# Attention layers and experts on one core: new issue orders, and layer 1 chunk by chunk across tiles

## The reference

```python
# 4 graphs, 512 nodes, 8 heads of 64, 4 experts
def gat_layer(x, adj, W, a_self, a_neigh, b):
    feat = jnp.einsum('nf,hfo->hno', x, W)
    e = leaky_relu(attn_self[:, :, None] + attn_neigh[:, None, :], 0.2)
    e = e + MASK_VAL * (1.0 - adj)[None, :, :]          # MASK_VAL = -1e10
    alpha = jax.nn.softmax(e, axis=-1)
    out = jnp.einsum('hnm,hmo->hno', alpha, feat) + b[:, None, :]
    return elu(out transposed to [n, h*o])
x = x + vmap(gat_layer twice)(ctx_512, layernorm(x))    # adj is the layer norm of x, [4, 512, 512]
x4 = layernorm(x).reshape(B, G, E, H)                   # row n goes to expert n % 4
gate, up = split(einsum('bgeh,ehd->bged', x4, gate_up_proj))
x = x + einsum('bgei,eih->bgeh', silu(gate) * up, down_proj).reshape(B, N, H)
```

## Time and profile before

| what | us |
|---|---|
| three runs | 219.91, 219.63, 218.56 |
| median | 219.63 |
| profiled execution, first to last instruction | 217.7 |
| PE busy in it | 204.2 |
| mean granted PE clock in it | 0.983 |

### The profile page before, as it was taken

The page is one execution under the profiler, slowest core; times in us unless marked ns, Lnnn a source line. Parts: engine busy times, 40 slices in busy tenths (PEclk is TensorE's granted clock), DMA queues, the critical chain, the costliest instruction groups (busy, mean ns, idle before and its releaser), DMA issues.

```text
span 217.7 us, 2718 instructions
## 1 busy us (share of the span) xinstructions
PE 204.2 (94%) x890; PEld 160.1 (74%) x890; DVE 151.1 (69%) x298; ACT 103.3 (47%) x159; POOL 102.7 (47%) x82
## 2 busy tenths in 40 slices
PE   7897899959999999999999999999999999999990
PEld 2346677836788888888888888888888888888860
DVE  0769999738999853999967857999788651610140
ACT  3899999958967431132183044762353032112100
POOL 2000968398887768897079110786044502202200
PEclk9999999979999999999999999999999999999996
DMA  6999879444552859779996446734991200230024
GB/s 209 335 427 401 271 251 403 167 96 97 102 135 29 213 117 241 107 139 176 260 382 234 161 176 227 249 155 117 336 376 42 98 0 0 82 114 0 0 83 120
DMA packets 15203, 38.80 MB, mean 178 GB/s; under 512 B 2768, under 2 KB 2768, under 8 KB 14160
## 3 DMA queue, kind: packets, MB, share of 16 engines
q1 hardware_dynamic: 12080, 34.10, 43.6%
q0 software_dynamic: 2816, 4.20, 13.1%
q10 hardware_dynamic: 288, 0.26, 0.4%
HBM read 30.16 MB, written 8.40 MB: 177 GB/s over the span
## 4 chain that ended last, share of the span: by engine, by line
PE 78%; DVE 8%; ACT 7%; POOL 2%; issue 1%; DMA 1%; ACTq 0%; POOLq 0%
PE bank L1696 30%; PE bank L1710 15%; PE bank L1657 10%; PE bank L1632 10%; PE bank L1683 5%; PE bank L1646 3%; PE bank L1620 2%; ACT hexp L933 2%; DVE found L1256 2%; DVE hexp L1227 2%; DVE top L1252 2%; DVE val L1246 2%; PE bank L1740 2%; ACT hexp L939 1%; DMA y_table<-val 1%
## 5 line engine op out<-in xcount | busy, mean ns | idle before, releaser
L1696 PE MATMUL bank<-acts,ring 128*128 128x512 f32 x288 | 67.2, 390 | 0.0
L1696 PEld LDWEIGHTS bank<-acts,ring 128*128 128x128 f32 x288 | 53.9, 188 | 11.1
L1632 PE MATMUL bank<-wide,acts 128*128 128x512 f32 x192 | 49.1, 409 | 5.3 <-POOL acts L801 2.4
L1632 PEld LDWEIGHTS bank<-wide,acts 128*128 128x128 f32 x192 | 36.2, 191 | 17.6 <-issue 5.0
L795 POOL TENSOR_TENSOR ring<-ring_raw,ring 128x1024 fp32r<-128x1024 f32 x13 | 32.2, 2491 | 31.8 <-ACT ring L926 31.8
L1710 PE MATMUL bank<-ring,wide 128*128 128x512 f32 x144 | 34.7, 392 | 0.0
L926 ACT CAST ring<-ring_raw 128x1024 fp32r<-128x1024 f32 x24 | 24.7, 1056 | 17.0 <-DMA ring_raw<-in_down_t 10.9
L1710 PEld LDWEIGHTS bank<-ring,wide 128*128 128x128 f32 x144 | 26.8, 188 | 5.3
L820 POOL DMA_INDIRECT x_sb<-y_table,ff_row x16 | 25.1, 1569 | 4.5 <-issue 3.9
L1657 PE MATMUL bank<-ring,first_xnT 128*128 128x512 f32 x96 | 23.2, 394 | 0.0
L1307 DVE TENSOR_TENSOR hexp<-bank,hexp 128x512 f32<-128x512 f32 x12 | 8.2, 684 | 20.7 <-PE bank L1696 20.7
(11 more groups left out here) (86 smaller groups left out, 243.6 us busy)
## 6 DMA issues: line engine op xcount, KB each, us to landing
ring_raw<-in_gate_up_t SPq DMA_DIRECT2D x16, 512.0 KB, 5.8
x_sb<-in_x SPq DMA_DIRECT2D x4, 1024.0 KB, 10.0
ring_raw<-in_down_t SPq DMA_DIRECT2D x8, 512.0 KB, 5.5
y_table<-val SPq DMA_DIRECT2D x16, 256.0 KB, 3.4
out<-x_sb SPq DMA_DIRECT2D x16, 256.0 KB, 2.8
val<-in_x SPq DMA_DIRECT2D x4, 1024.0 KB
ctxT<-in_ctx_t SPq DMA_DIRECT2D x4, 256.0 KB, 5.2
wide_raw<-in_W_t SPq DMA_DIRECT2D x2, 512.0 KB, 7.0
```

The lines of the kernel that those rows point to most:

```text
L1632: last = nc.tensor.matmul(bank[Y_BANK[n]][:, :], hT[:, b % 2, c, w, t * P:(t + 1) * P], W1p[:, c, v, :], start=False, stop=(c == KC - 1 an ...
L1696: last = nc.tensor.matmul(bank[(UP_BANK if half else GATE_BANK)[KC * e + c]][:, :], ring[:, r % RING, w, col:col + P], xnT[:, (e - 1) % 2, ...
```

## The change

Nothing is added to or taken from the work: each engine has the same computing instructions and transfers as before, in a new order, with other waits and banks. (An unused helper, `keep_on`, goes.) What moves:

- SP loads `ctx` 1, both halves of W1 and b1 first, then x and the ring slots mixed, and all nine slots, all of x and all of `ctx` are issued before `store_y(0)`. The re-reads of the check are spread otherwise between the later ring loads.
- ACT runs `w_high(1)`, `seed(0)`, `w_high(2)` ahead of the first `h_exp_of`. DVE runs both `w_low` ahead of its first `h_below`.
- PE issues layer 1 by `layer1_part`, chunk by chunk with up to four tiles open at a time, and the waits on `w_lo` and `h_lo` move out of `layer1_part` to the list.
- The first expert's calls come in another order: `first_up` and `first_down` earlier, `turn_xn` singly between matmuls.
- All bank tables change, and the count of sure rows goes to `SURE_BANK` 5.

```diff
-        Z_BANK = (7, 1, 4, 3, 2, 1, 5, 3, 7, 1, 0, 2, 0, 4, 7, 5)
-        Y_BANK = (6, 4, 6, 5, 3, 4, 1, 5, 7, 6, 1, 2, 7, 2, 1, 2)
+        Z_BANK = (0, 2, 3, 4, 5, 6, 0, 2, 3, 4, 4, 1, 7, 4, 1, 2)
+        Y_BANK = (1, 7, 5, 6, 0, 1, 7, 2, 5, 6, 0, 3, 7, 4, 1, 2)
...
             load_ctx(0)
+            load_ctx(1)
             load_w(1)
-            load_ctx(1)
+            load_b1(0)
+            load_w(2)
+            load_x(2)
             load_ctx(2)
-            load_b1(0)
+            load_x(0)
+            load_r(1)
             load_x(1)
-            load_w(2)
-            load_x(0)
             load_r(0)
-            load_x(2)
+            load_x(3)
+            load_r(3)
+            load_r(5)
+            load_ctx(3)
+            load_r(2)
             load_r(8)
-            load_r(1)
-            load_r(2)
+            load_r(7)
+            load_r(4)
+            load_r(6)
             store_y(0)
-            load_r(7)
-            load_r(5)
-            load_r(6)
             store_y(1)
             store_f(0)
             store_y(2)
-            load_r(4)
             store_y(3)
-            load_r(3)
-            load_ctx(3)
-            load_x(3)
+            store_f(1)
...
             h_low(1, 3)
-            r_low(2)
-            h_low(2, 0)
             follow(0, 0)
             follow(0, 1)
+            follow(1, 0)
+            h_low(2, 0)
             follow(0, 2)
+            r_low(2)
             gather(0, 0)
+            r_low(4)
             h_low(2, 3)
             gather(0, 1)
-            r_low(4)
-            follow(1, 0)
+            h_low(3, 0)
+            gather(1, 0)
+            h_low(3, 1)
...
+            w_high(1)
+            seed(0)
+            w_high(2)
             h_exp_of(0, 0)
-            w_high(1)
             h_exp_of(0, 1)
...
+            w_low(1)
+            w_low(2)
             h_below(0, 0)
             h_value(0, 0)
-            w_low(1)
             h_below(0, 2)
...
                 if c == 0:
                     pe.wait_ge(y_seeded, n + 1)
-                if t == 0:
-                    wait_h_lo(pe, KC * b + c)
-                if n == 0 and c % 2 == 0:
-                    pe.wait_ge(w_lo, 1 + c // 2)
...
             layer0(1, 0)
-
+            layer0(1, 1)
+            pe.wait_ge(h_made, 1)
+            layer0(1, 2)
             pe.wait_ge(h_made, 2)
-            layer0(1, 1)
-            layer0(1, 2)
-
+            layer0(1, 3)
+            pe.wait_ge(h_made, 3)
+            layer0(2, 0)
+            pe.wait_ge(w_lo, 1)
+            wait_h_lo(pe, 0)
             layer1_part(0, 0)
+            layer1_part(1, 0)
+            wait_h_lo(pe, 1)
+            layer1_part(1, 1)
             pe.wait_ge(h_made, 4)
-            layer0(1, 3)
+            layer0(2, 1)
             layer1_part(0, 1)
...
```

More of the change, by code:

```diff
@@ L766, in _ @@
             load_r(22)
-            again_x(3)
             load_r(23)
@@ L1088, in _ @@
+            r_high(4)
+            y_exp_of(7)
+            h_exp_of(3, 0)
             h_high(2, 2)
[L1089 removed]
+            h_below(3, 0)
             h_high(2, 3)
[L1091 to L1103 removed]
```

770 lines of the change are left out of this document (417 added, 353 removed).

## The result

The changed kernel takes 235.03 us (median of 4 runs, 234.31 to 236.33) against 219.09 of the kernel before on the same chip: ratio 1.074, 95% interval 1.068 to 1.080. It is 16 us slower. The profiled execution is the slowest of the four, 236.33 us; its span is 234.5 us (before 217.7), its mean granted clock 0.95 (before 0.983).

The account below looks back on a forecast made before the run. PE was taken as the bound, with 10.1 us lost, nearly all before 50 us. Profiled span 217.7 minus 3.9 us of gain (clock falling at the start) gave 213.8; plus 1.9 us carried over, 215.7 us, range 212.8 to 220.8.

Parts of the forecast that it names:

- The change behind 68 us: Experts' stage after layer 1: work comes 4 us earlier, its feeders keep up with margins of 0 to 1 us.
- the sum of these: Net cost of the small margins in the experts' stage: zero, with up to 2 us in the range.
- 115.0 against 114.7 to 116: Experts' stage: r_low(9) behind x2_inverse(3, 2) comes at 115.0 us, PE reaches it at 114.7 to 116.
- rival (c): A late feeder of the experts, likeliest output(1, 0) before 148.9 us, gives the gain back: 217.5 to 219.6 us; chance 0.2.
- The front: Kernel start: PE stands 3.8 us, until 13.8, for h_value(0, 0) behind both W1 halves, whose second lands at 10.2.
- The fall of the clock: Behind the first PE gap: 3.1 to 3.3 us at half rate, of which 1.3 us are really lost.
- 14 to 49 us: Layer 1 chunk by chunk: small waits of 0.2 us to 38, 0 to 0.3 us for h_low(2, 0), old gap gone.
- rival (d): Early weight loads delay the f_row 1 store, PE stands 5 us and the clock falls: 222.5 us; chance 0.16.
- 49 to 68 us: Rest of layer 1: low halves come before PE needs them; it ends at 66.9, or 68.2 with the clock.
- 0.6 us on chunk (3, 3): Layer 1: DVE's h_low takes twice as long beside a POOL step, some 0.6 us, leaving 0.3 us of margin.
- 10.1 us is all that any order can give: Whole kernel: PE uses 206.9 us for 196.8 us of work, so reordering can win at most 10.1 us.
- rival (b): Start loads beat the walk, W1 landing at 9 instead of 10.2: 1.2 us more gain, 213 us; chance 0.08.

Follow-up runs that it names:

- experiment 7: Experiment 1 with x2_stats(2, 0) moved behind normalize(1, 2) on DVE: 224.96 us, ratio 1.026.
- experiment 6: Changed kernel with 44 small dummy matmuls on PE in the first gap to hold the clock up: 234.82 us, ratio 1.071.
- experiment 1: Changed kernel with only all_maxima moved back to its old place behind r_low(12) on POOL: 226.59 us, ratio 1.032.
- experiment 4: Changed kernel with r_low(4) behind h_low(2, 3) on POOL: uneven runs of 231.57, 231.92, 235.61 and 236.43 us.
- experiment 9: Experiments 1, 4 and 7 together, with r_low(9) and r_low(10) also ahead of x2_inverse(2, 2) again: 228.04 us, ratio 1.035.
- experiment 16: Kernel before the change with h_low(2, 3) ahead of follow(0, 2) and gather(0, 0) on POOL: 218.23 us, ratio 0.995.
- experiment 17: Experiment 16 plus x2_stats(0, 0) behind y_value(8) on DVE and both h_low(3, ...) ahead of gather(1, 1) on POOL: 219.03 us, ratio 1.000.
- experiment 5: Changed kernel with both W1 halves behind the first chunks again on ACT and DVE, loads as changed: 233.98 us, ratio 1.069.
- experiment 12: Experiment 11 with ACT's and DVE's first steps also put back as in experiment 5: 225.85 us, ratio 1.032.
- experiment 14: Experiment 12 with gather(0, 1) between h_low(2, 3) and r_low(4) on POOL: 224.15 us, ratio 1.022.
- experiment 11: Changed kernel with experiments 1, 4 and 7 together, r_low(9) left where the change put it: 221.94 us, ratio 1.011.

## Why the prediction was wrong

It said 215.7 us (212.8 to 220.8) and 0.67 for faster; it is 235.03 and slower. The failed step is "The change behind 68 us", and in it the sentence "I put the sum of these at zero and up to 2 us in the range": 14.9 us were lost there, 0.5 in the kernel before.

- **`all_maxima`** was never priced, though the move stands in the diff and the two holes in POOL's timeline of the kernel before (5.80 us "issue" in front, everything behind covered by a wait for ACT). Seen from PE it cost nothing there, and what covered it was not looked at. Undoing it alone gives 8.4 us, replacing the instruction 6.7.
- **`x2_stats(2, 0)`** ahead of `normalize(0, 3)` stands in front of a wait of 1.83 us; that it costs them is not shown, since moving it alone only moved the wait (experiment 7). **`r_low(9)`** behind `x2_inverse(3, 2)` cost 1.81 us once it was exposed. For `r_low(9)` the prediction had its margin as 115.0 against 114.7 to 116. Two waits of this size are rival (c)'s kind, but not at the place where it looked, and no row names `output(1, 0)`.
- **The clock behind the third gap:** 4.5 us at 0.50, in which PE loses 2.3 us, a wait of 0.43 among them. The prediction had no term for it there.
- **The front** had the right mechanism and a wrong size: gap until 13.8 predicted, 15.16 measured; 5.3 us lost predicted, 7.5 measured at 22 us. W1's second half landed at 11.65, not 10.2: bytes queued ahead of it were the only term, between two landings of the earlier trace rows. An earlier landing would not have helped either: `seed(0)` stands ahead of `w_high(2)` and needs b1, which landed at 10.3, and the bias row and the seed kept ACT busy until 11.64; the prediction had no term for these 1.3 us of work. The fall of the clock was right, its price nearer 2 us than 1.3 (experiment 6). Fronts with the same lists differ by up to 2 us between executions (lost at 22 us: 7.5, 7.8, 6.0, 6.2 and 7.9 in the changed kernel and experiments 1, 4, 7 and 9), so this term wanted a range of 2 us by itself.
- **14 to 49 us** went as walked: no wait for a `seed`, `w_lo` or `h_lo`, 7.5 to 7.6 us lost. The old wait at 44 us is gone, `h_low(2, 0)` behind `follow(1, 0)` costs nothing, and rival (d), loads ahead of `f_row`, did not happen.
- **49 to 68 us** failed at chunk (2, 2). The prediction had the mechanism, put it at 0.6 us on chunk (3, 3) and kept the sum. DVE's operation took 4.7 times its length (3.15 us), PE waited 2.34 us and then ran at the low clock. The prediction treated the overlap as a slow-down by two, when the operation can be held until two POOL instructions in a row are through.
- **The accounting**, "10.1 us is all that any order can give", nearly all of it lost before 50 us, was right as a bound and wrong as a forecast. In the kernel before, experiments 16 and 17 win 2.1 us by 46 us and 4.1 us by 61 us and keep 0.6 and 0.5. In the changed kernel the traces of experiments 4 and 5 keep what they won by the end of layer 1 (4.8 and 1.8 us), but other runs of the same lists are slower, and the medians are only 1.3 and 1.0 us lower. Undoing the front beside the other repairs even cost time (experiments 12 and 14 against 11), though 2.3 us less were lost at 22 us (6.4 and 4.1 in experiments 11 and 12): by the end of layer 1 experiments 11 and 14 both stand at 7.6.
- **The range.** Half-way from the forecast of 215.7 to rival (d)'s 222.5 is 219.1, not 220.8, and rival (b) gives 213.2, not 212.8. Neither changes the outcome.

What stays open: 2.5 us of the 16 (experiment 11 is still 1.1% slower), of which 1.8 are the wait for `r_low(9)`, behind the `x2_inverse` on POOL; the spread between runs of one list; and what makes the hole in front of a reduction 5.6 us long or 11.7. That `all_maxima` at the new place in the kernel before does the same was not tried: there `small_maxima` stands behind `normalize(2, 2)` on DVE, and the two would wait for each other.

## What to carry to other kernels

Before a step is moved, list on its engine what surrounds it in the trace, "issue" holes included, and ask what hides them at the old place and who waits right behind the new one; a call that cost PE nothing may have taken 14 us of a queue that nobody needed. Where several orders were moved together, undo them with their partners (a load, its cast, its low half): `r_low(9)` and `r_low(10)` alone at their old place cost 5 to 6 us (experiment 9 against 11, by ratio and by median). And a gain made upstream can end at the next engine that is just in time, as in experiments 16 and 17, so price the first two waits behind it before adding it up.
